# Cross-attention on one core: the query job ahead of the first key chunk, the inversion at key tiles 4 to 7, the product in halves, the output jobs at key tiles 10 and 12

## The reference, cut to what matters

```python
q = (x @ W_q)            # 512 queries, heads of 64
k = (context @ W_k)      # 1601 keys
v = (context @ W_v)
sim = einsum('bihd,bjhd->bhij', q, k) * 64 ** -0.5     # layer 0: masked keys out
attn = softmax(sim, axis=-1)
out = einsum('bhij,bjhd->bihd', attn, v).reshape(b, n, INNER)
x = x + out @ W_o + b_o
```

## Time and profile before

| | us |
|---|---|
| median of 3 runs | 3351.64 (3348.53 to 3357.45) |
| the profiled execution | 3356.66 |
| its span | 3354.9 |
| PE busy | 2927.0 (87%) |
| DVE busy | 1919.5 (57%) |
| POOL busy | 1678.3 (50%) |
| ACT busy | 1318.5 (39%) |
| granted clock, mean | 0.937 |

### The profile page before, as it was taken

The page is one execution under the profiler, slowest core; times in us unless marked ns, Lnnn a source line. Parts: engine busy times, 40 slices in busy tenths (PEclk is TensorE's granted clock), DMA queues, the critical chain, the costliest instruction groups (busy, mean ns, idle before and its releaser), DMA issues. The chain is left out here.

```text
span 3354.9 us, 38241 instructions
## 1 busy us (share of the span) xinstructions
PE 2927.0 (87%) x12634; PEld 1718.1 (51%) x12634; DVE 1919.5 (57%) x3738; ACT 1318.5 (39%) x2299; POOL 1678.3 (50%) x1408
## 2 busy tenths in 40 slices
PE   6578786899899999687589999999999999999979
PEld 5323334545455455353455555555555555555457
DVE  2456675666756656433555665566556555655546
ACT  1134452444444444311144444444444444444420
POOL 0344202565656656610246666666666666666620
PEclk8778897999999999897699999999999999999979
DMA  8666503222322312000222232222322223222110
GB/s 270 146 156 151 136 1 87 67 79 65 72 76 59 98 41 54 34 0 0 81 57 58 65 99 58 60 65 64 94 53 65 70 61 84 67 63 58 38 51 26
DMA packets 113532, 245.81 MB, mean 73 GB/s; under 512 B 15366, under 2 KB 61703, under 8 KB 112184
## 3 DMA queue, kind: packets, MB, share of 16 engines
q1 hardware_dynamic: 107128, 219.82, 26.3%
q0 software_dynamic: 5696, 23.42, 2.5%
q10 hardware_dynamic: 512, 0.13, 0.0%
HBM read 107.31 MB, written 31.76 MB: 41 GB/s over the span
## 5 line engine op out<-in xcount | busy, mean ns | idle before, releaser
L1000 POOL TENSOR_TENSOR ACC<-ACC,PR 128x512 f32<-128x512 f32 (+1 forms) x1056 | 1347.4, 1299 | 610.6 <-ACT PR L1174 610.1
L1174 ACT ACTIVATE PR<-banks 128x512 f32<-128x512 f32 (+1 forms) x832 | 485.8, 597 | 715.7 <-PE banks L1088 713.9
L1233 DVE TENSOR_REDUCE mx<-banks 128x2 f32<-128x800 f32 (+1 forms) x512 | 508.1, 992 | 293.9 <-PE banks L1059 287.7
L1105 PE MATMUL banks<-PR,V 128*64 128x512 f32 (+1 forms) x2496 | 666.7, 617 | 0.1
L1059 PE MATMUL banks<-KH,QZ 128*128 128x400 f32 (+1 forms) x1536 | 496.0, 378 | 132.8 <-DVE mx L1230 46.4
L1087 PE MATMUL banks<-QA,KA 128*128 128x512 f32 (+1 forms) x1248 | 553.8, 444 | 4.6 <-DMA QB<-ROW 4.6
L1088 PE MATMUL banks<-QB,KB 65*128 65x512 f32 (+1 forms) x1248 | 494.7, 396 | 0.0
L1203 DVE TENSOR_TENSOR KB<-banks,KH 64x400 fp32r<-64x400 f32 (+1 forms) x384 | 219.6, 572 | 440.1 <-ACT KH L1133 434.7
L1059 PEld LDWEIGHTS banks<-KH,QZ 128*128 128x128 f32 x1536 | 273.2, 190 | 375.7 <-issue 172.0
L1087 PEld LDWEIGHTS banks<-QA,KA 128*128 128x128 f32 (+1 forms) x1248 | 230.4, 185 | 375.2 <-issue 283.0
L1174 ACT ACTIVATE PR<-banks,keybias 128x512 f32<-128x512 f32 (+1 forms) x416 | 274.8, 687 | 364.1 <-PE banks L1088 349.9
(11 more groups left out here) (228 smaller groups left out, 3018.4 us busy)
## 6 DMA issues: line engine op xcount, KB each, us to landing
KA<-KH SPq DMA_DIRECT2D x192, 400.5 KB, 6.1
CX<-ctx_split SPq DMA_DIRECT2D x8, 2403.0 KB, 10.5
WK<-wk_split SPq DMA_DIRECT2D x48, 256.0 KB, 5.7
WV<-wv_split SPq DMA_DIRECT2D x24, 512.0 KB, 3.7
QA<-QZ SPq DMA_DIRECT2D x96, 128.0 KB, 2.3
QB<-QZ SPq DMA_DIRECT2D x96, 128.0 KB, 2.4
first<-in_w_in SPq DMA_DIRECT2D x8, 1024.0 KB, 6.0
second<-in_w_out1T SPq DMA_DIRECT2D x8, 1024.0 KB, 8.9
```

Of the source, the lines that this page charges most:

```text
L1000: pool.tensor_tensor(acc, other, PR[0:r, n % RING, :], ALU.add).then_inc(summed, 1)
L1105: last = pe.matmul(OB[h * DH:(h + 1) * DH, :], V[0:r, g % 4, s, h * DH:(h + 1) * DH], PR[0:r, (n + h) % RING, :], start=(s == 0), stop=(s ...
L1174: act.activation(PR[0:r, n % RING, :], SB[n % 3][0:r, :], ACT.Exp, bias=keybias[0:r, g // pairs, t:t + 1] if masked else 0.0).then_inc(pro ...
L1233: dve.tensor_reduce(mx[:, :, t, c], both[:, :, 0:w], AX.X, ALU.max).then_inc(mx_done, 1)
```

## The change

Four edits, all in `cross`:

1. In key tile 0 the query job of the next group comes before its first key chunk. In layer 1, where a key tile has a single maximum it moves from place 0 to place 2, behind the jobs; layer 0's table is shifted in the same sense.
2. The four inversions go from key tiles 2 to 5 to key tiles 4 to 7.
3. The product with the inverted sums goes from key tile 6, one instruction of 512 columns, to key tiles 8 and 9, two of 256 columns; "out" 0 waits for the first alone.
4. The output jobs go from key tiles 8 and 9 to 10 and 12, the first ahead of the row job (t = 11) and the second behind it.

```diff
@@ at(g, t)
-                jobs += {0: [("k", g + 1, 0), ("q", g + 1, 0)], 1: [("k", g + 1, 1)], 2: [("k", g + 1, 2)],
+                jobs += {0: [("q", g + 1, 0), ("k", g + 1, 0)], 1: [("k", g + 1, 1)], 2: [("k", g + 1, 2)],
...
-            if g >= 1 and t in (8, 9):
-                jobs.append(("out", g - 1, t - 8))
             if g + 1 < G and t == 11:
                 jobs.append(("row", g + 1, 0))
+            if g >= 1 and t in (10, 12):
+                jobs.append(("out", g - 1, (t - 10) // 2))
...
-            where = spread({1: 2, 2: 3, 3: 3, 4: 3, 5: 4, 6: 4, 7: 4, 8: 3, 9: 3, 10: 3},
-                           {2: (1, 3), 3: (0, 2, 3), 4: (0, 1, 2, 3)})
+            where = spread({1: 2, 2: 3, 3: 3, 4: 3, 5: 3, 6: 4, 7: 3, 8: 4, 9: 4, 10: 3},
+                           {2: (2, 3), 3: (0, 2, 3), 4: (0, 1, 2, 3)})
...
-            where = spread({1: 1, 2: 1, 3: 1, 4: 2, 5: 2, 6: 2, 7: 2, 8: 2, 9: 2, 10: 1}, {1: (0,), 2: (0, 2)})
+            where = spread({1: 1, 2: 1, 3: 1, 4: 2, 5: 2, 6: 2, 7: 2, 8: 2, 9: 2, 10: 1}, {1: (2,), 2: (0, 2)})
@@ TensorE, job "out"
-                            pe.wait_ge(normed, g + 1)
+                            pe.wait_ge(normed, 2 * g + c + 1)
@@ ScalarE, job "sum"
-                                act.wait_ge(normed, g)
+                                act.wait_ge(normed, 2 * g)
@@ VectorE
-                    def normalise(g):
+                    def normalise(g, i):
+
+                        half = slice(i * S // 2, (i + 1) * S // 2)
                         dve.wait_ge(inverted, NT * (g + 1))
                         dve.wait_ge(o_done, g + 1)
-                        dve.tensor_tensor(OT[:, :], OT[:, :], RD[:, :], ALU.mult).then_inc(normed, 1)
+                        dve.tensor_tensor(OT[:, half], OT[:, half], RD[:, half], ALU.mult).then_inc(normed, 1)
...
-                            if g >= 1 and 2 <= t < 2 + NT:
-                                invert(g - 1, t - 2)
-                            if g >= 1 and t == 2 + NT:
-                                normalise(g - 1)
+                            if g >= 1 and 4 <= t < 4 + NT:
+                                invert(g - 1, t - 4)
+                            if g >= 1 and t in (8, 9):
+                                normalise(g - 1, t - 8)
```

More of the change, by code:

```diff
@@ L1305, in _ @@
                         invert(G - 1, i)
-                    normalise(G - 1)
+                    for i in range(2):
+                        normalise(G - 1, i)
                     for x in after:
```

## The result

| | us |
|---|---|
| before, median of 4 runs | 3354.55 (3348.53 to 3360.80) |
| changed, median of 4 runs | 3523.49 (3519.55 to 3527.04) |
| ratio, with its 95% interval | 1.0503 (1.0479 to 1.0528) |
| span of the profiled execution, changed | 3517.8 |

The change makes the kernel 169 us slower. The forecast was 3486, 134 slower, with a range to 3528. The page of the changed kernel: its first line, and part 1 with busy time and share of each engine.

What follows compares the result with a forecast made beforehand. The prediction took TensorE's queue to set the time. Its terms, 8 + 19 + 43 - 19 + 22 + 46 + 15 = +134 us on the median of 3351.6, gave 3486 us, with a range of 3435 to 3528.

Steps and rivals of the forecast that it cites:

- Bound: TensorE's queue: Cross-attention: TensorE's queue sets the time; other engines count only where TensorE waits for them.
- The row transfer without WV, 0.9 in 24 groups: Group's end, both layers: ROW issued behind WO lets TensorE start 0.75 late, plus 0.15 for weights; +22 us.
- The row transfer behind WV, 2.3 in 20 groups: Group's end, both layers: ROW queued behind WO and WV costs 2.3, between bounds 1.3 and 2.6; +46 us.
- The clock, +15: After the wait behind WV: TensorE's clock falls, costing 1.5 each time, in half of 20 groups; +15 us.
- the rival of a fall at nearly every group's start: Group starts: 34 more clock falls than counted, at 1.5 each; +185, 3537 us; chance 0.11.
- Query job first, +8: Start of layer 1's groups: the wait passes to key chunk 1, +0.25 a group in 31 groups; +8 us.
- The first maximum of tile 4, +19: Layer 1, tile 4: first maximum now behind key chunk 3's subtraction on DVE, net +0.6 in 31 groups; +19 us.
- The output jobs, +43: Layer 1: output jobs at tiles 10 and 12 cost their full 0.8 each, +1.6 in 27 groups; +43 us.
- Layer 0, -19: Layer 0: two long waits each shrink by an inversion, the start gets worse; net -1.35 in 14 groups, -19 us.
- the passing ROW: Rival: ROW passes WV and the clock holds, 1.3 lost in 20 groups; +99, 3451 us; chance 0.17.
- the hidden one: Rival: the row wait is hidden, as SP lets ROW go early or PVs cover it; +51, 3403 us; chance 0.03.
- the faster kernel: Rival: VectorE's order was the whole trouble, moved inversions remove the waits in both layers; -30, 3322 us; chance 0.04.

Runs made afterwards that it cites:

- f1: The changed kernel with only SP's order differing: WV, then ROW, then the wait for the second output job and WO; 3424.03 us, ratio 1.0204.
- f2: The changed kernel with SP's order WO, ROW, WV, ROW still waiting for the second output job; 3444.35 us, ratio 1.0279.
- g1: The kernel before with inversions at tiles 4 to 7, product in halves at 8 and 9, output jobs at 9 and 10; 3328.63 us, ratio 0.9920.

## Why the prediction was right, and where it was off

The direction, the order of the parts and each place named in the trace came out; the time, 3523, lies at the upper end of the range, 37 above the number. Every term had the right sign; four were too small, and the short row wait and layer 0's gain were put too large. Put in as measured, they come to 163: 16 for the query job, 18 for tile 4, 47 for the output jobs, -15 for layer 0, 15 and 55 for the row transfer, 27 for the clock. The 6 up to the 169 of the medians are within their scatter.

- *Bound: TensorE's queue.* Right. The terms that were put on it appear in the groups' lengths.
- *The row transfer without WV, 0.9 in 24 groups.* The mechanism is right, the size was high: 0.59 in the bracket and 0.64 by the groups' lengths. The score started 0.59 late and not 0.75, and the 0.15 for a reload of weights is 0.04. That is -7 on the sum.
- *The row transfer behind WV, 2.3 in 20 groups.* The mechanism is shown by f1 and f2, the size was low: 2.71 on the mean in brackets (68.3 less 24 x 0.59, over 20), 2.75 by the groups' lengths, beyond my upper bound of 2.6. The step that failed is the bound itself: I let ROW land together with WV, 3.7 us after WV's issue, but the score started at 4.04. That is +9 on the sum.
- The Trainium skill ("DMA: Bandwidth & Descriptors", "Queues, rings and completion order") says that each DMA engine takes descriptors in ring order. The runs agree: TensorE waited 2.7 us for a ROW behind WV and 0.6 for one ahead of it. Of the Trainium skill's other statement there, that completion is not first in, first out, nothing showed in a transfer of 4 KB behind one of 512.
- *The clock, +15.* Right in kind, low: the groups' lengths put 27 on it (29 against f2). The step that failed is the half: the clock fell behind 18 of the 20 long waits, not 10. The 1.5 for a fall was about right (29 over 18), and the rival of a fall at nearly every group's start did not come. By the rows, the long wait is followed by a granted clock of 0.66 over 5 us, the short one by 1.00. The Trainium skill ("TensorE: Matmul & The Clock Gate", "The HAM clock gate") says that the gate goes by how busy TensorE has been, which agrees in direction.
- *Query job first, +8.* The failing step is that I let the maximum of tile 1 cost nothing new. Key chunk 1 lost the 1.35 that I had worked out (1.18 + 0.16 here), but the maximum moved behind the jobs no longer runs in that wait's shadow. From the query job's start to PV of tile 1 it takes 7.67 us in f1. Before, key chunk 0 was the first of these jobs, 0.92 ahead of the query job, and from its start to PV it took 7.14. So +0.53, not +0.25: 16 us.
- *The first maximum of tile 4, +19.* Right in size: the tile takes 5.08 us in f1 and took 4.49 before, +0.59 against +0.6.
- *The output jobs, +43.* Right: in f1 tile 10 is 3.38 us long and tile 12 3.82, where their lengths were 2.5 and 2.95, 0.87 each, while tiles 8 and 9 keep theirs because the wait took the job's place (0.72 and 0.62 in brackets). 1.74 in 27 groups is 47.
- *Layer 0, -19.* Right, a little large (its own working gives -1.30 a group, not -1.35). A group of layer 0 without V jobs takes 46.24 us in f1 and up to 47.73 before, and the waits on L1230 fell by 24 us; but over the 14 groups f1 is only 14.6 us shorter.

The two stretches of f1, a group of layer 0 and one of layer 1, which carry these sums (the latter 2.90 longer than the earlier trace rows; 0.25 + 0.6 + 1.6 = 2.45 was expected):

```profile
679.27:725.51 46.24, 43.57 (x175) 23.15 (x173) 32.02 (x83) 21.82 (x36) 30.60 (x24) 1.00 0.42 115
2268.00:2318.82 50.82, 47.52 (x215) 27.91 (x214) 28.68 (x35) 21.67 (x40) 30.55 (x24) 1.00 0.24 54
```

Of the rivals, the passing ROW is refuted by f2, the hidden one and the faster kernel by the page. But the last had a true part: what it said of layer 0's inversions is part of a change worth 28 us when the output jobs go no further than tiles 9 and 10 (g1).

## What to carry to other kernels

A job has two prices: its own time, and what it hides. The output jobs were free where they stood, because a wait for a free bank was due there anyway, and cost their full time two tiles later; a maximum cost nothing inside the wait for QA and its full time behind it. And when a step is moved, look at every queue that waits for it by name: SP waited for the output job to free a buffer whose next reader came nearly two groups later, with the one transfer that TensorE did need standing behind it. Reordering that queue (f1) gave back 99 of the 169 us.

## What the runs showed of the hardware

A 4 KB transfer issued 0.42 us behind one of 512 KB on the same queue let its reader start 3.62 us after its own issue, against 2.05 behind a 128 KB one, and 1.98 in the group of the earlier trace rows, where WV had left 3.49 us before it; with the 512 KB behind it, it was as fast as without. I had not expected it to be later than the big transfer's own 3.7 us. And TensorE's clock kept 1.00 through waits of 0.6 and 1.2 us a few us apart in each of 42 groups (f2), while behind a wait of 2.63 us it was 0.66 over 5 us; 18 of the 20 groups that follow a wait of 2.56 us or more ran below 1.00. An idle time in brackets is not always short of the loss by the same amount: a wait of 2.62 for ROW cost 2.67, one of 0.78 for a bank cost 1.04.
